# Moving the signals of TensorE onto drains in five attention passes of a graph network

## The reference, cut to what matters

```python
scores = jnp.sum(q_dst * kt, axis=-1) / scale       # 8 heads; with 4 heads: leaky_relu(el[src] + er[dst])
m = jax.ops.segment_max(scores, dst, num_segments=N)
e = jnp.exp(scores - m[dst])
s = jax.ops.segment_sum(e, dst, num_segments=N)
w = e / (s[dst] + 1e-10)
agg = jax.ops.segment_sum(V[src] * w[..., None], dst, num_segments=N)
```

## Time and profile before

| | |
|---|---|
| median of 3 runs | 7653.98 us (7653.26 to 7665.72) |
| span of the profiled execution | 7518.3 us |
| own time of the profiled execution | not shown apart from the span; the median is 135.7 us above the span |
| PE busy | 4867.8 us (65%), 24003 matmul records |
| weight loads busy | 3723.3 us (50%) |
| DVE busy | 3884.0 us (52%) |
| ACT busy | 3561.5 us (47%) |
| GpSimd busy | 3734.9 us (50%) |
| mean granted clock of TensorE | 0.736 |

### The profile page before, as it was taken

The page is one execution under the profiler, slowest core; times in us unless marked ns, Lnnn a source line. Parts: engine busy times, 40 slices in busy tenths (PEclk is TensorE's granted clock), DMA queues, the critical chain, the costliest instruction groups (busy, mean ns, idle before and its releaser), DMA issues. The chain is left out here.

```text
span 7518.3 us, 87581 instructions
## 1 busy us (share of the span) xinstructions
PE 4867.8 (65%) x24003; PEld 3723.3 (50%) x24003; DVE 3884.0 (52%) x9168; ACT 3561.5 (47%) x8843; POOL 3734.9 (50%) x3964
## 2 busy tenths in 40 slices
PE   4444445447775677657767886677896777796444
PEld 3444333324553445445555774555694555574332
DVE  7222222235665566756667436666545666573233
ACT  2333232224444444455555564555575555454555
POOL 1655466646663566245555235555224555314665
PEclk6555566666767677787777997777897777798676
DMA  1111233333442344255556125555325555423333
GB/s 59 47 47 47 72 93 91 92 88 108 109 109 71 102 108 110 68 174 163 172 164 161 58 97 160 166 169 166 77 68 162 165 174 167 126 79 114 93 91 91
DMA packets 392076, 841.54 MB, mean 112 GB/s; under 512 B 92953, under 2 KB 203451, under 8 KB 388163
## 3 DMA queue, kind: packets, MB, share of 16 engines
q0 software_dynamic: 209680, 603.03, 28.9%
q1 hardware_dynamic: 173696, 228.71, 9.6%
q10 hardware_dynamic: 8243, 4.30, 0.2%
HBM read 727.80 MB, written 107.96 MB: 111 GB/s over the span
## 5 line engine op out<-in xcount | busy, mean ns | idle before, releaser
L700 POOL DMA_INDIRECT ring<-tab_kv,idx_i x1392 | 1322.0, 950 | 1172.1 <-PE pp L769 578.5
L943 DVE TENSOR_TENSOR acc<-acc,pp 128x264 f32 x1576 | 670.6, 425 | 942.3 <-DMA WE<-in_L_gnn_W_E 339.3
L700 POOL DMA_INDIRECT ring<-tab_z,src_i x880 | 842.0, 957 | 541.3 <-issue 237.5
L769 PE MATMUL pp<-ring,X 128*128 128x264 f32 x2784 | 946.4, 492 | 200.1 <-issue 162.0
L1126 PE MATMUL pp<-ring,oh 128*128 128x256 f32 x1760 | 598.9, 499 | 639.7 <-DMA bb<-in_L_gnn_b 221.5
L726 PE MATMUL pq<-Qs,oht 128*128 x6816 | 813.0, 257 | 257.7 <-issue 162.8
L726 PEld LDWEIGHTS pq<-Qs,oht 128*128 128x128 bf16 x6816 | 636.2, 109 | 506.4 <-issue 320.9
L1260 DVE TENSOR_TENSOR acc<-acc,pp 128x256 f32 x880 | 370.3, 421 | 882.4 <-remote 275.8
L1126 PEld LDWEIGHTS pp<-ring,oh 128*128 128x128 f32 x1760 | 419.2, 251 | 819.8 <-issue 465.1
L769 PEld LDWEIGHTS pp<-ring,X 128*128 128x128 f32 x2784 | 629.8, 241 | 351.8 <-issue 203.4
L769 PE MATMUL pp<-ring,scratch 128*128 128x264 f32 x1760 | 648.0, 510 | 128.5 <-issue 68.2
(11 more groups left out here) (356 smaller groups left out, 8992.6 us busy)
## 6 DMA issues: line engine op xcount, KB each, us to landing
oht<-lo_row_p SPq DMA_DIRECT2D x174, 256.0 KB
tab_kv<-X SPq DMA_DIRECT2D x100, 384.0 KB
oht<-lo_row_s SPq DMA_DIRECT2D x110, 256.0 KB
drow<-in_dst SPq DMA_DIRECT2D x25, 1024.0 KB
tab_h<-hs SPq DMA_DIRECT2D x25, 1024.0 KB, 4.4
ring<-tab_kv,idx_i POOLq DMA_INDIRECT x1392
tab_kv<-room SPq DMA_DIRECT2D x50, 384.0 KB, 3.0
ring<-tab_z,src_i POOLq DMA_INDIRECT x880
```

Source lines behind the costliest of these rows:

```text
L700: nc.gpsimd.indirect_dma_start(out=ring[:, w % RW, c, :], out_offset=None, in_=table, in_offset=bass.IndirectOffsetOnAxis(ap=idx[:, w * WC ...
L769: last = nc.tensor.matmul(pp[n % NB][:, 0:W8], oh[:, w % 2, UC * n + c, :], ring[:, w % RW, UC * n + c, 0:W8], start=(c == 0), stop=(c == ...
L943: nc.vector.tensor_tensor(a, a, pp[p % NB][:, 0:W8], ALU.add).then_inc(s_acc, 1)
```

## The change

Every increment that PE makes in the passes moves from the matmul or transpose to a drain instruction right behind it. A drain holds PE's sequencer until the engine has finished what was issued. In all there are 4 quarters, 16 units and 6 other signals a window in a pass over sums (2, 8 and 6 in the half window), and 4, 8 and 6 in a pass over dots: 718 drains in each of two passes and 522 in each of three, 3002 together. Nothing else changes.

```diff
                             for r in range(3):
-                                last = nc.tensor.matmul(o, lhs, Qs[:, bass.ds(tile_, 1), r, :].rearrange("p a d -> p (a d)"),
-                                                        start=(r == 0), stop=(r == 2))
-                        last.then_inc(s_q, 1)
+                                nc.tensor.matmul(o, lhs, Qs[:, bass.ds(tile_, 1), r, :].rearrange("p a d -> p (a d)"),
+                                                 start=(r == 0), stop=(r == 2))
+                        nc.tensor.drain().then_inc(s_q, 1)
...
-                        nc.tensor.transpose(sc_t, scw[:, w % 2, :, :].rearrange("p h c -> p (h c)"), ident[:, :]).then_inc(s_T1, 1)
+                        nc.tensor.transpose(sc_t, scw[:, w % 2, :, :].rearrange("p h c -> p (h c)"), ident[:, :])
+                        nc.tensor.drain().then_inc(s_T1, 1)
...
-                        nc.tensor.matmul(diff, neg_i[:, :], R, start=False, stop=True).then_inc(s_sub, 1)
+                        nc.tensor.matmul(diff, neg_i[:, :], R, start=False, stop=True)
+                        nc.tensor.drain().then_inc(s_sub, 1)
...
-                                         start=True, stop=True).then_inc(s_Gm, 1)
+                                         start=True, stop=True)
+                        nc.tensor.drain().then_inc(s_Gm, 1)
...
-                        nc.tensor.transpose(sc_t, S1, ident[:, :]).then_inc(s_T4, 1)
+                        nc.tensor.transpose(sc_t, S1, ident[:, :])
+                        nc.tensor.drain().then_inc(s_T4, 1)
                         e.wait_ge(s_eg, w + 1)
-                        nc.tensor.transpose(ex_t, S1, ident[:, :]).then_inc(s_T5, 1)
+                        nc.tensor.transpose(ex_t, S1, ident[:, :])
+                        nc.tensor.drain().then_inc(s_T5, 1)
...
-                        nc.tensor.matmul(fac, first_row, gr[:, :], start=False, stop=True).then_inc(s_fac, 1)
+                        nc.tensor.matmul(fac, first_row, gr[:, :], start=False, stop=True)
+                        nc.tensor.drain().then_inc(s_fac, 1)
...
                         for c in range(UC):
-                            last = nc.tensor.matmul(pp[n % NB][:, 0:W8], oh[:, w % 2, UC * n + c, :], ring[:, w % RW, UC * n + c, 0:W8],
-                                                    start=(c == 0), stop=(c == UC - 1))
-                        last.then_inc(s_pp, 1)
+                            nc.tensor.matmul(pp[n % NB][:, 0:W8], oh[:, w % 2, UC * n + c, :], ring[:, w % RW, UC * n + c, 0:W8],
+                                             start=(c == 0), stop=(c == UC - 1))
+                        nc.tensor.drain().then_inc(s_pp, 1)
```

## The result

The changed kernel takes 8537.85 us (median of 4 runs, 8521.16 to 8560.62) against 7653.62 us (7634.04 to 7665.72, 4 runs): 1.1163 times as long, with a 95% interval of 1.1143 to 1.1184. That is +884 us where +802 was forecast. The profiled execution took 8532.84 us with a span of 8531.1. In each of these four runs the time is within 2 us of the span, so the profiled execution of the kernel before (span 7518.3) was a shorter one than those behind its median. I therefore compare windows, not spans.

The account below looks back on a forecast made before the run. It took waits inside the five passes, not any engine's total work, as the bound. Drains would add 672 us over sums and 130 over dots, 802 on 7654: told as 8450 us, range 7780 to 8850.

Parts of the forecast that it names:

- The path over sums: PE's serial work in a window over sums: 35.8 us at the low clock against 23.8, +672 us over 56 windows.
- The 0.11 us for drain and next issue: Price of each drain on PE's sequencer together with the next issue, with bounds 0.05 and 0.25 us.
- The clock over sums: PE's clock in passes over sums, taken as low (0.50): 35.8 us a window, against 27.1 at the high clock.
- The other, smaller price of a unit: From the Trainium skill's fixed matmul cost: a unit alone pays 0.29 us, not 0.49; some 180 us less over sums.
- Over dots the term: A window over dots goes from 27.9 to 29.5 us, +1.5 us on 87 windows, +130 us.
- The guess that it stays: Over dots PE's late signals stay in part, a little under half kept: a window of 29.5 us instead of 27.3.
- Rival (c): A drain's signal escapes the lateness of PE's signals in windows of both kinds, so faster: 7142 us; chance 0.11.
- (a): PE's clock stays high in passes of both kinds: 7790 to 8140 us; chance 0.16.
- (b): PE's clock stays low in passes of both kinds: 9006 us, or over 8800; chance 0.14.
- (d): The drain does not hold PE and weight loads still run ahead: 7690 us or no change; chance 0.07.
- The sum: Windows over sums and over dots together: 672 + 130 = 802 us more, told as 8450 us; chance 0.52.
- the forecast of the profiled span: The whole kernel's span in the profile goes from 7518.3 to some 8320 us.

Follow-up runs that it names:

- units only: The changed kernel with drains kept behind the units alone, all other signals back on their matmuls: 6912.06 us, where the kernel before takes 6204.
- dense quarters: The changed kernel with 12 more bf16 matmuls, never read, in each quarter over sums: 7257.89 us, against 7405.65 for the changed kernel again.
- bare drains: The changed kernel with each signal back on its matmul and a drain without a signal behind it: 7409.10 us, against 7405.65 for the changed kernel again.

## Why the prediction was right, and where a term was off

- **The path over sums**: 35.8 forecast, 35.1 measured. Term by term in the first trace: units 1.32 us each for 1.36; a quarter with its drain 1.77 for 1.7 (its register work comes into the open by the drain of the unit ahead, as the run with units only shows); `below` to the first transpose of `T4` 1.61 for 1.7 + 0.45, since the exponential lies beside `ratio`; from there to `factor`'s end 2.84 for 3.0; tile numbers 1.50 for 1.4. The 0.11 us for drain and next issue was 0.08.
- **The clock over sums**: the low level was taken, and the granted clock was 0.50. The other, smaller price of a unit that the prediction named, by which the sum would have been 180 us lower, does not show: a drained unit grew by 0.45 us (0.87 to 1.32), not by 0.29. A unit alone at the low clock has a record of 1.24 us, 1.25 in rows 3. At the high one a drained unit comes every 0.79 us (weight loads at 1830.47 and 1831.26 in the kernel with dense quarters), where 0.82 was forecast.
- **Over dots the term was mis-sized**: "If nothing of the 5.57 us is mended the window is near 33; I keep a little under half: 29.5". It was 32.2, +357 us and not +130. Two errors lie in it, of opposite sign. The path without lateness is 25.0 us and not 27.3: I had taken `T4` to `factor` and `below` with `ratio` from rows at the low clock, 3.0 and 1.5 + 0.45 us. Over dots, at the high one, they take 1.9 (5600.45 to 5602.38) and 1.1 (5631.96 to 5633.06), in the first trace of the changed kernel:

```profile
5600.45 0.33 PE L749 MATMUL pc<-ident,X 128*128 128x128 f32 x1
...
5602.02 0.36 PE L761 MATMUL pc<-gr,X 1*128 1x8 f32 x2
...
5631.96 0.49 PE L737 MATMUL pc<-ident,scw 128*128 128x128 f32 x2 [0.65 <-DVE X L918]
...
5633.06 0.33 PE L749 MATMUL pc<-ident,X 128*128 128x128 f32 x1
```

  And the lateness costs 7.2 us a window and not 2.2: the drain is no cure, because it ends as late and holds PE's queue as well.
- **The guess that it stays was right in kind and less than a third in size** (2.2 for 7.2 us). I argued from rows 5, where a drain has no tail, that a drain's price is small, and from their place at a pass's end that they say nothing of its middle. The second was true: in the middle of a pass over dots a drain lasted up to 7.7 us, and at the start of a pass, which the sum left out, up to 31.3. I had also read 5.57 us of idle DVE as lateness, though the last unit was recorded as ended 3.3 us before the addition (4030.77 and 4034.05).
- **Rival (c)** was true for a part. Over sums the late signals, 3.7 us a window, did vanish: without them the drains cost 15.0 us there, and in the result 11.3. Over dots nothing vanished. Over sums the loss was larger than the gain, as its price had it.
- **Rivals (a), (b) and (d)** fell: clock 0.50 over sums and 0.80 over dots; bare drains cost as much as signalling ones.
- **The sum**: 672 + 130 = 802 us forecast, 633 + 357 = 990 by the profiled windows, 884 by the medians. The profiled execution of before was 2% shorter than the timed ones, so the windows of its trace overstate the change by some 100 us, and the forecast of the profiled span, 8320 us, which stood on it, was 211 too low. That the medians stand nearer the forecast than the windows do is luck.

**What stays open** is why completions were late in the first measurement. There a window over dots has the lateness with and without drains, a window over sums only without, and the start of every pass has it in both kernels. In the later sessions it is never there. At the starts of passes it goes with GpSimd's fetches, but the same fetches in the later sessions leave PE on time. No kernel here turned it on or off, so neither its cause nor why the drains ended it inside the windows over sums is shown.

## What to carry to other kernels

A drain behind a group of matmuls costs little by itself (0.08 us here); it costs the overlap of the next group's weight load and register work with this one's end (a quarter behind a drained unit took 1.6 us for 0.5), and that is paid in full only when the engine has no waiting time left: the quarters' drains were free alone and 163 us in company. If a drain must be there, put few of them (one for two units gave back 278 us) and put scalar reads between the last matmul and the drain (147 us). And look whether the groups that are left raise the clock: some work added in nearly empty stretches made this kernel faster.

## What the runs showed of the hardware that was not expected

- The same kernel, with the same durations of DVE's and ACT's instructions, took 7654 us in one session and 6204 in three others on three chips. In the attention passes the difference lies largely in idle time behind work that PE's records show as done.
- A drain can end long after the last matmul that it waits for: 4.6 us in the window shown, up to 6.8 inside passes over dots, and 31 at the start of a pass, while GpSimd issued 64 indirect DMAs. Its end there is the end that the other engines see, so the modelled end of a matmul is no proof that the engine has been told.
- A drain on an idle engine has a record of 13 ns and delays the next issue by 80.
- A chain of single fp32 units with 0.08 us between their records, PE busy 828 of 1050 us, kept the clock at 0.50 through a whole pass.
